# State-space kernel summed on TensorE, split gate product, and output products between gates, in the first stage of a decoder layer

## The chip, the cores and the metric

One core of a Trainium2 chip runs the whole program. The metric is the device time in microseconds of one execution; the median of three runs is given, and one further execution was profiled.

## What is computed

The program is one decoder layer on x of 8 batches x 512 steps x 256: a state-space (Mamba) block, a cross attention over 64 context rows, and a mixture of experts. The change lies in the first block. Its convolution branch is multiplied by zero, so that the input of the recurrence is 1 everywhere:

```python
xc = xc * 0 + 1
dBC = xc @ W_x.T
delta = jax.nn.softplus(dlt @ W_dt.T + b_dt)
A = -jnp.exp(A_log)
h = dA * h + dBx          # step, dA = exp(d_t * A)
y = ys.transpose(1, 0, 2) + D_skip * xc
out = y * jax.nn.silu(z) @ W_out.T
```

So y depends on the step t and on the inner channel alone (512 channels, 16 states each): with rate r = delta * A and coefficient c = B * C * delta of a channel's states, y(t) is D plus the running sum over t of the sum over 16 states of c * exp(r * t). z = x_norm @ W_in differs by batch.

## The kernel before, in words

All work is in 128-partition tiles. A batch is four tiles of 128 steps (TB = 4), the model width two blocks of 128 (KD = 2), the inner width four (KE = 4). The first stage (the functions under `nc.Block()`, lines 214 to 561) is written out by hand as one instruction order for each engine, with semaphores between them. For every batch b it does this.

- VectorE takes the statistics (`stats_part`, L111 and L115), GpSimd the inverse deviation (`norm_rstd`, L120 and L122), and each of them normalises two tiles (`norm_apply`, L127). The normalised tiles `hn`, the statistics and the deviation have one buffer each.
- TensorE transposes them (`transposes`, L274), ScalarE copies the result to SBUF (`evac`, L479), and `z_part` (L287) makes z with plain fp32 matmuls. z is copied out by ScalarE for three of four blocks (L484) and by VectorE for the fourth (L420), and kept for all eight batches in `sz`.
- Beside it the state-space kernel is summed: 64 times (4 channel blocks x 16 states) ScalarE makes 511 exponentials (`pw`, L500) and VectorE adds them into `kern` with their coefficient (L424). A scan over `kern` then gives `yD` (L429).
- When all of z is there, TensorE makes the keys' values (L314, and L315 with the bias as a product of one row), then the output products: `out_part(b)` waits for the low part of the gated z. VectorE multiplies z (after silu) with `yD` (`gate`, L440), ScalarE makes the high part `gh` (`high`, L512), VectorE the low part `gl` (`low`, L141), TensorE 48 products of 256 columns (`product`, L135 to L137), VectorE adds them to x (`residual`, L436). Output banks are two, so batch b waits for the residual of batch b - 1.
- GpSimd then lays the keys out in blocks (`kbd`, L555) for the next stage.

A split operand is a pair of fp32r tensors, high and low; `product` multiplies such pairs in three matmuls (high by high, high by low, low by high). An fp32 matmul shows as two records in the trace.

The last instruction of the stage on VectorE is the second residual of batch 7. All engines meet there, and the attention stage begins.

## Time and profile before

| | us |
|---|---|
| median of 3 runs | 992.65 (989.8 to 994.75) |
| the profiled execution, own time | 989.96 |
| its span | 988.3 |
| TensorE busy (matmul) in the span | 923.4 |
| VectorE busy | 625.2 |
| ScalarE busy | 556.4 |
| GpSimd busy | 347.0 |

Busy time of a matmul includes its pipelined end, so that neighbours overlap and the spacing of their starts is the pace. "Idle before" in a row is the time for which the engine had nothing to do, with what ended it. The first stage ends at about 166 us; the lines changed by the edit are all in it, save the preparation of inputs on the host.

### The profile page before, as it was taken

The numbers are of one execution on the slowest core, as the hardware profiler recorded it, in microseconds if no ns is written. First come the engines' busy times: TensorE is split into PE (matmuls) and PEld (weight loads), VectorE is DVE, ScalarE is ACT, GpSimd is POOL, SyncE is SP. The second block draws the span as 40 slices with busy tenths as digits, with TensorE's granted clock in tenths as the row PEclk, the third lists the DMA queues.
The fourth block names the chain that finished last, engine by engine and source line by source line (L and its number), as shares of the span: only waits on it lengthen the run. The fifth ranks groups of instructions, "written<-read, shape, count | busy, mean of one in ns | idle before, by whom it ended". The sixth has DMA issues, their size and how long they took to land.

```text
span 988.3 us, 20180 instructions
## 1 busy us (share of the span) xinstructions
PE 923.4 (93%) x6832; PEld 792.9 (80%) x6833; DVE 625.2 (63%) x1485; ACT 556.4 (56%) x1109; POOL 347.0 (35%) x323
## 2 busy tenths in 40 slices
PE   2998898799999889999999999999999999999996
PEld 2444697455666468888888889999999999999996
DVE  4898897566775666666665566546565646565453
ACT  3688842365545454444644467557565657565552
POOL 3652723222120235555555322424233332423222
PEclk9999999999999999999999999999999999999998
DMA  9200002000000201111112843534325252523222
GB/s 254 92 1 1 1 1 72 21 1 1 1 1 1 94 1 67 68 67 67 68 67 76 264 116 94 134 49 107 66 44 131 42 140 44 130 42 54 44 44 33
DMA packets 49312, 64.21 MB, mean 65 GB/s; under 512 B 10289, under 2 KB 42290, under 8 KB 49138
## 3 DMA queue, kind: packets, MB, share of 16 engines
q0 software_dynamic: 17504, 34.87, 15.2%
q1 hardware_dynamic: 31618, 27.68, 9.6%
q10 hardware_dynamic: 144, 1.05, 0.4%
q8 instruction: 28, 0.46, 0.2%
q14 instruction: 18, 0.15, 0.1%
HBM read 38.82 MB, written 24.77 MB: 64 GB/s over the span
## 4 chain that ended last, share of the span: by engine, by line
PE 71%; DVE 7%; ACT 3%; issue 1%; DMA 0%; POOL 0%; SPq 0%; DVEq 0%; POOLq 0%; ACTq 0%
PE PS L135 20%; PE PS L136 19%; PE PS L137 19%; PE PS L646 3%; DVE mxpad L897 2%; PE PS L1559 2%; PE PS L687 2%; PE PS L673 2%; PE PS L693 1%; ACT recs L802 1%; ACT prT L783 1%; PE PS L1109 1%; DVE mxT L908 1%; DMA xr<-routed_rows 0%; DVE hidl L141 0%
## 5 line engine op out<-in xcount | busy, mean ns | idle before, releaser
L1605 ACT ACTIVATE hideh<-PS,be 128x256 fp32r<-128x256 f32 x280 | 140.5, 502 | 152.4 <-PE PS L137 152.4
L1633 POOL DMA_INDIRECT out_rows<-y,toki x70 | 122.3, 1747 | 268.3 <-DVE y L1673 259.1
L141 DVE TENSOR_TENSOR hidel<-act32e,hideh 128x256 fp32r<-128x256 f32 x280 | 118.4, 425 | 107.9 <-ACT act32e L1607 107.6
L135 PE MATMUL PS<-xTeh,wfch 128*128 128x256 f32 x560 | 159.4, 285 | 2.2 <-issue 1.1
L136 PE MATMUL PS<-xTel,wfch 128*128 128x256 f32 x560 | 158.5, 283 | 0.0
L137 PE MATMUL PS<-xTeh,wfcl 128*128 128x256 f32 x560 | 158.4, 283 | 0.0
L135 PE MATMUL PS<-wprh,hideh 128*128 128x256 f32 x560 | 157.9, 282 | 0.0
L137 PE MATMUL PS<-wprh,hidel 128*128 128x256 f32 x560 | 154.8, 277 | 0.0
L136 PE MATMUL PS<-wprl,hideh 128*128 128x256 f32 x560 | 154.8, 277 | 0.0
L1607 ACT ACTIVATE act32e<-PS,be 128x256 f32<-128x256 f32 x280 | 140.9, 503 | 2.8 <-DVE hidel L141 2.8
L135 PEld LDWEIGHTS PS<-xTeh,wfch 128*128 128x128 f32 x560 | 107.3, 192 | 3.8 <-issue 2.3
L137 PEld LDWEIGHTS PS<-xTeh,wfcl 128*128 128x128 f32 x560 | 107.5, 192 | 0.0
L136 PEld LDWEIGHTS PS<-xTel,wfch 128*128 128x128 f32 x560 | 107.3, 192 | 0.0
L136 PEld LDWEIGHTS PS<-wprl,hideh 128*128 128x128 f32 x560 | 105.3, 188 | 0.0
L135 PEld LDWEIGHTS PS<-wprh,hideh 128*128 128x128 f32 x560 | 105.2, 188 | 0.0
L137 PEld LDWEIGHTS PS<-wprh,hidel 128*128 128x128 f32 x560 | 105.2, 188 | 0.0
L1218 ACT ACTIVATE hidh<-PS,bfs 128x512 fp32r<-128x512 f32 x64 | 44.2, 690 | 57.8 <-PE PS L137 54.2
L120 POOL TENSOR_TENSOR vare<-mv,small 128x4 f32<-128x4 f32 x24 | 9.0, 376 | 189.4 <-DVE mv L115 189.2
L1291 POOL DMA_INDIRECT routed_rows<-rows,slotc x64 | 65.5, 1024 | 24.9 <-issue 19.3
L135 PE MATMUL PS<-wpsh,hidh 128*128 128x256 f32 x256 | 73.5, 287 | 0.3 <-DVE hidl L141 0.3
L137 PE MATMUL PS<-wpsh,hidl 128*128 128x256 f32 x256 | 72.1, 282 | 0.0
L136 PE MATMUL PS<-wpsl,hidh 128*128 128x256 f32 x256 | 72.1, 282 | 0.0
(254 smaller groups left out, 2165.3 us busy)
## 6 DMA issues: line engine op xcount, KB each, us to landing
xr<-routed_rows SPq DMA_DIRECT2D x36, 272.0 KB, 2.8
fcraw<-in_Wfc POOLq DMA_DIRECT2D x8, 1024.0 KB, 6.0
prraw<-in_Wproj POOLq DMA_DIRECT2D x8, 1024.0 KB, 8.6
X<-in_x SPq DMA_DIRECT2D x8, 512.0 KB, 6.1
out_rows<-X SPq DMA_DIRECT2D x8, 512.0 KB, 3.0
routed_rows<-pads SPq DMA_DIRECT2D x8, 272.0 KB, 4.5
out_rows<-y,toki POOLq DMA_INDIRECT x70, 3.8
ctx<-in_ctxT SPq DMA_DIRECT2D x4, 256.0 KB
```

The costliest lines, as they stand in the source:

```text
L135: nc.tensor.matmul(out, wh, xh, start=first, stop=False)
L136: nc.tensor.matmul(out, wh, xl, start=False, stop=False)
L137: return nc.tensor.matmul(out, wl, xh, start=False, stop=last)
L141: return eng.tensor_tensor(out, whole, high.bitcast(F32), ALU.subtract)
L646: last = nc.tensor.matmul(at, qT[rows, b % 2, m, t * P:(t + 1) * P], kbd[rows, b, m, :].rearrange("p (i n) -> p i n", i=2), start=m == 0, ...
L673: nc.tensor.matmul(PS[:, j, :], kbd[rows, b, m, j % 2 * P:(j % 2 + 1) * P], qT[rows, b % 2, m, :], start=True, stop=False, skip_group_chec ...
L687: last = nc.tensor.matmul(PS[32 * j:32 * j + 32, 2, :], onesbd[:, m, :], prT[:, m, j, :], start=m == 0, stop=m == KD - 1, skip_group_check ...
L1218: nc.scalar.activation(hid[0][:, j, :], PS[:, j % 4, :], ACT.Gelu_apprx_tanh, bias=bfs[:, j:j + 1])
L1291: nc.gpsimd.indirect_dma_start(out=RG, out_offset=bass.IndirectOffsetOnAxis(ap=slotc[:, t, m:m + 1], axis=0), in_=rows[:, t, :], in_offset ...
L1605: nc.scalar.activation(hid[0][:, j, :], PS[:, j % 4, 0:BLK], ACT.Gelu_apprx_tanh, bias=bias)
L1607: nc.scalar.activation(act32[:, j % 2, :], PS[:, j % 4, 0:BLK], ACT.Gelu_apprx_tanh, bias=bias).then_inc(h_ready, 1)
L1633: nc.gpsimd.indirect_dma_start(out=out, out_offset=bass.IndirectOffsetOnAxis(ap=toki[:, h:h + 1], axis=0), in_=y[:, h, :], in_offset=None, ...
```

## The change

The state-space kernel is no longer made state by state. exp(r t) is factored as exp(r (t mod 64)) times exp(r 64 (t div 64)): `powers` holds 64 + 8 exponentials for each of 64 channel groups (8 channels x 16 states on the partitions), made from products with `steps` (`arguments` on VectorE, `powers_exp` on ScalarE, four chunks). `columns` puts the coefficient and a mask of the channel in. 64 matmuls (`kernel_sums`) contract over the 128 partitions, ScalarE copies the sums out (`kernel_rows`), and 32 transposes (`kernel_turn`) bring channels onto partitions; `response` scans from PSUM. The z product takes split operands (`winp`; `hTh` by ScalarE, `hTl` by VectorE in `x_low`). z of batches 4 to 7 is made after the output products of batches 0 to 3, in five buffers instead of eight; batches 3 to 7 take silu straight out of PSUM. VectorE's rounds begin with the residual. The value bias is folded into the bias `bo` by two matmuls at the end. x of batch 0 is loaded first. VectorE normalises three of four tiles of the first five batches. The key blocks lie between GpSimd's rounds.

```diff
-        SLOT = KE * NS // B
-        PWB = 4
+        NE = P // NS
+        G = EI // NE
+        GH = G // 2
+        NA = 8
+        NB = L // NA
+        SLOTS = 5
+        BY_DVE = [3] * 5 + [2] * (B - 5)
...
+            CHUNKS = [slice(16 * i, 16 * (i + 1)) for i in (0, 2, 1, 3)]
+            COPIED = 3
...
-                    for dst, src in ((wx[:], d["W_xT"].rearrange("(k p) r -> p k r", p=P)),
-                                     (wdt[:], d["W_dtT"]), (bdt[:], d["b_dt"]), (dsk[:], d["D_skip"]),
-                                     (alog[:], d["A_log"].rearrange("(k p) n -> p k n", p=P)),
-                                     (steps[:], d["steps"])):
-                        sp.dma_start(dst, src).then_inc(w_in, 16)
                     x_load(0)
                     for dst, src in ((ident[:], d["ident"]), (small[:], d["small"])):
                         sp.dma_start(dst, src).then_inc(consts_in, 16)
+                    for dst, src in ((wx[:], d["W_xT"].rearrange("(k p) r -> p k r", p=P)),
+                                     (wdt[:].rearrange("r e g -> r (e g)"), d["W_dtT"]), (bdt[:], d["b_dt"]),
+                                     (dsk[:], d["D_skip"]), (alog[:], d["A_log"]), (steps[:], d["steps"])):
+                        sp.dma_start(dst, src).then_inc(w_in, 16)
...
-                    def z_part(b):
-                        pe.wait_ge(hT_ready, KD * b + KD)
-                        for e in range(KE):
+                    def z_part(b, parts=range(KE)):
+                        pe.wait_ge(hT_low, KD * b + KD)
+                        for e in parts:
                             if b:
-                                if e < KE - 1:
-                                    pe.wait_ge(z_copied[0], (KE - 1) * (b - 1) + e + 1)
-                                else:
-                                    pe.wait_ge(z_copied[1], b)
+                                pe.wait_ge(z_copied, KE * (b - 1) + e + 1)
+                            if b == 3 and e < KD:
+                                pe.wait_ge(kT_ready, e + 1)
+                            if b == 3 and e >= KD:
+                                pe.wait_ge(yD_ready, 2)
+                            if b == 4:
+                                pe.wait_ge(v_ready, 4 * (e + 1))
                             for k in range(KD):
-                                last = nc.tensor.matmul(PS[:, e, :], win[:, k, e * P:(e + 1) * P],
-                                                        hT[:, b % 2, k, :], start=k == 0, stop=k == KD - 1)
+                                last = product(PS[:, e, :], [w[:, k, e * P:(e + 1) * P] for w in winp],
+                                               [x[:, b % 2, k, :] for x in (hTh, hTl)], k == 0, k == KD - 1)
                             last.then_inc(z_psum, 1)
 
-                    pe.wait_ge(consts_in, 32)
-                    transposes(0)
...
-                    for b in range(B):
-                        z_part(b)
-                        if b < B - 2:
-                            transposes(b + 2)
...
+                    def kernel_sums(half):
+                        pe.wait_ge(cU_ready, 2 * half + 2)
+                        if half:
+                            pe.wait_ge(ksb_ready, half)
+                        for q in range(GH // 2):
+                            for j in range(2):
+                                g = GH * j + GH // 2 * half + q
+                                last = nc.tensor.matmul(PS[NB * j:NB * (j + 1), 6 + q // 8, q % 8 * NB:(q % 8 + 1) * NB],
+                                                        powers[:, g, 0:NB], cU[:, g, :], start=True, stop=True,
+                                                        skip_group_check=True)
+                        last.then_inc(raw_psum, 1)
+
+                    def kernel_turn(half):
+                        pe.wait_ge(ksb_ready, half + 1)
+                        bank = (2, 6)[half]
...
+                        for a in range(NA):
+                            for j in range(2):
+                                rows = slice(NB * j, NB * (j + 1))
+                                last = nc.tensor.transpose(PS[:, bank + j, a * NB:(a + 1) * NB], ksb[rows, half, a, :],
+                                                           ident[rows, rows])
+                        last.then_inc(kern_psum, 1)
...
+                    transposes(0)
+                    pe.wait_ge(dlt_ready, 1)
+                    for e in range(NE):
+                        last = nc.tensor.matmul(PS[0:G, 6, 8 + e:9 + e], wdt[:, e, :], dlt[:], start=True, stop=True)
+                    last.then_inc(small_mm, 1)
+                    pe.wait_ge(win_split, 2)
+
+                    def z_and_transposes(b):
+                        z_part(b, range(KE - 1))
+                        transposes(b + 1)
+                        z_part(b, range(KE - 1, KE))
+
+                    z_and_transposes(0)
+                    pe.wait_ge(rates_ready, 1)
+                    for i, src in enumerate((rate, coef)):
+                        last = nc.tensor.transpose(PS[:, 7, P + G * i:P + G * (i + 1)], src[:], ident[0:G, 0:G])
+                    last.then_inc(small_mm, 1)
+                    z_and_transposes(1)
+                    kernel_sums(0)
+                    z_and_transposes(2)
+                    kernel_sums(1)
+                    keys()
+                    kernel_turn(0)
+                    kernel_turn(1)
+                    z_and_transposes(3)
+                    values()
                     for b in range(B):
                         out_part(b)
+                        if b + 5 < B:
+                            transposes(b + 5)
+                        if b + 4 < B:
+                            z_part(b + 4)
+                    pe.wait_ge(bv_ready, 1)
+                    for k in range(KD):
+                        last = nc.tensor.matmul(PS[:, 0, 0:D], bv[:, k, :], wo[:, k, :], start=k == 0, stop=k == KD - 1)
+                    last.then_inc(bo_psum, 1)
...
+                    def x_low(b):
+                        if b >= 2:
+                            dve.wait_ge(z_psum, KE * (b - 1))
+                        for k in range(KD):
+                            dve.wait_ge(hT_high, KD * b + k + 1)
+                            low(nc.vector, hTl[:, b % 2, k, :], PS[:, 4 + k, :], hTh[:, b % 2, k, :]).then_inc(hT_low, 1)
+
+                    def arguments(i):
+                        gs = CHUNKS[i]
+                        nc.vector.tensor_tensor(powers[:, gs, :],
+                                                rcT[:, 0, gs].unsqueeze(2).to_broadcast([P, 16, NB + NA]),
+                                                steps[:].unsqueeze(1).to_broadcast([P, 16, NB + NA]),
+                                                ALU.mult).then_inc(prod_ready, 1)
+
+                    def columns(i):
+                        gs = CHUNKS[i]
+                        dve.wait_ge(powers_ready, i + 1)
+                        nc.vector.tensor_tensor(cU[:, gs, :].rearrange("p g (a e) -> p g a e", e=NE),
+                                                cmask[:, gs, :].unsqueeze(2).to_broadcast([P, 16, NA, NE]),
+                                                powers[:, gs, NB:].unsqueeze(3).to_broadcast([P, 16, NA, NE]),
+                                                ALU.mult).then_inc(cU_ready, 1)
+
+                    def response(half):
+                        dve.wait_ge(kern_psum, half + 1)
+                        bank = (2, 6)[half]
+                        for j in range(2):
+                            k = 2 * j + half
+                            nc.vector.tensor_tensor_scan(yD[:, k * L:(k + 1) * L], onesrow[:], PS[:, bank + j, :],
+                                                         dsk[:, k:k + 1], ALU.mult, ALU.add).then_inc(yD_ready, 1)
 
...
+                    x_low(1)
+                    stats_part(2)
+                    dve.wait_ge(small_mm, 3)
+                    link(nc.vector.tensor_copy(rcT[:].rearrange("p i g -> p (i g)"), PS[:, 7, P:P + 2 * G]))
+                    arguments(0)
+                    apply_part(2)
+                    arguments(1)
+                    link(nc.vector.tensor_tensor(cmask[:], rcT[:, 1, :].unsqueeze(2).to_broadcast([P, G, NE]),
+                                                 emask.unsqueeze(1).to_broadcast([P, G, NE]), ALU.mult))
+                    stats_part(3)
+                    columns(0)
+                    columns(1)
+                    x_low(2)
+                    arguments(2)
+                    apply_part(3)
+                    arguments(3)
+                    stats_part(4)
+                    columns(2)
+                    columns(3)
+                    x_low(3)
+                    apply_part(4)
+                    response(0)
+                    response(1)
                     dve.wait_ge(yD_ready, KE)
+                    stats_part(5)
                     gate(0)
+                    dve.wait_ge(wout_split, 1)
+                    low(nc.vector, wouts[1][:], wout[:], wouts[0][:]).then_inc(wout_split, 1)
+                    gate(1)
+                    x_low(4)
+                    gate_low(0)
+                    gate(2)
                     for b in range(B):
-                        if b < B - 1:
-                            gate(b + 1)
-                        dve.wait_ge(g_high, b + 1)
-                        low(nc.vector, gl[:, b, :], sz[:, b, :], gh[b % 2][:]).then_inc(g_low, 1)
                         if b:
                             residual(b - 1)
+                        if b + 5 < B:
+                            apply_part(b + 5)
+                        if b + 3 < B:
+                            gate(b + 3)
+                        if b + 1 < B:
+                            gate_low(b + 1)
+                        if b + 6 < B:
+                            stats_part(b + 6)
+                        if b == 4:
+                            dve.wait_ge(late_in, LATE_IN)
+                            nc.vector.tensor_copy(causal16[:], causal[:])
+                            nc.vector.tensor_copy(ident16[:], ident[:])
+                            nc.vector.tensor_copy(bv[:], bvc[:].unsqueeze(2).to_broadcast([P, KD, P])).then_inc(bv_ready, 1)
                         if b == B - 2:
-                            dve.wait_ge(x1_ready, 2 + 2)
+                            for half in hn_ready:
+                                dve.wait_ge(half, B)
                             norm_stats(link, tiles(0)).then_inc(hn_var, 1)
-                        if b == B - 1:
-                            dve.wait_ge(hn_rstd, 2 * B + 2)
-                            norm_apply(0)
+                        if b + 5 < B:
+                            x_low(b + 5)
+                    dve.wait_ge(hT_psum, B)
+                    dve.wait_ge(hn_rstd, 2 * B + 2)
+                    norm_apply(0)
                     residual(B - 1)
-                    dve.wait_ge(x1_ready, 2 * B + 2)
+                    dve.wait_ge(bo_psum, 1)
+                    nc.vector.tensor_tensor(bo[:], bo[:], PS[:, 0, 0:D], ALU.add).then_inc(bo_ready, 1)
+                    dve.wait_ge(x1_ready, 2 * B)
```

TensorE's queue from its third group of products on, before. `PS` is PSUM, `hT` the transposed x, `win` the weights of z, `ctx` the context, `wk` the key weights.

```order
L263 MATMUL PS<-dlt,wdt 128x1 x4
L274 MATMUL PS<-ident,hn 128x128 x16
L287 MATMUL PS<-hT,win 128x512 x8
L274 MATMUL PS<-ident,hn 128x128 x8
L287 MATMUL PS<-hT,win 128x512 x8
L274 MATMUL PS<-ident,hn 128x128 x8
L304 MATMUL PS<-ctx_79,wk 128x512 x4
L287 MATMUL PS<-hT,win 128x512 x8
```

And now, TensorE around the second half of the sums (between z of batch 2 and z of batch 3):

```order
L137 MATMUL PS<-hTh,winl 128x512
L302 MATMUL PS<-cU,powers 64x64 x32
L326 MATMUL PS<-ctx_79,wk 128x512 x4
L317 MATMUL PS<-ident,ksb 128x64 x32
L135 MATMUL PS<-hTh,winh 128x512
```

Sixteen transposes stood together ahead of the first z; now eight do, and the sums, the keys and the turning transposes stand between z products (the first half of the sums, 32 more, stands between z of batches 1 and 2).

VectorE in the output rounds, before. `sz` is the gate product, `gl` the low part, `X` the residual.

```order
L440 TENSOR_TENSOR sz<-sz,yD 128x2048
L141 TENSOR_TENSOR gl<-sz,gh_101 128x2048
L436 TENSOR_TENSOR X<-X,PS 128x512 x2
L440 TENSOR_TENSOR sz<-sz,yD 128x2048
L141 TENSOR_TENSOR gl<-sz,gh_100 128x2048
L436 TENSOR_TENSOR X<-X,PS 128x512 x2
```

And now, one round of batches 1 to 2 and the beginning of the next:

```order
L459 TENSOR_TENSOR X<-X,PS 128x512 x2
L127 TENSOR_SCALAR hn<-X,mv,rstd 128x256 x2
L466 TENSOR_TENSOR sz<-sz,yD 128x2048
L141 TENSOR_TENSOR gl<-sz,gh_90 128x2048
L111 BN_STATS stats<-X 128x6 x4
L115 BN_AGGR mv<-stats 128x2 x4
L141 TENSOR_TENSOR hTl<-PS,hTh 128x512 x2
L459 TENSOR_TENSOR X<-X,PS 128x512 x2
```

The residual stands first, and normalising, statistics and the low part of a later batch's x lie in the round.

## Rows read from the trace of the kernel before

**Rows 1.** Stretches of z and output products: length, PE, PEld, DVE, ACT, POOL busy, PEclk.
```profile
28.20:97.60 69.40, 66.64 (x187) 32.25 (x186) 61.23 (x129) 56.82 (x99) 32.14 (x24) 0.98 0.05 16
...
112.40:164.90 52.50, 49.68 (x384) 48.92 (x384) 42.80 (x40) 26.03 (x20) 20.36 (x18) 0.94 0.00 1
```

**Rows 2.** Timeline to 30 us: start us, us, engine line op out<-in xcount [idle before].
```profile
0.89 0.46 SPq L225 DMA_DIRECT2D wx<-in_W_xT  x1
...
4.14 0.43 SPq L218 DMA_DIRECT2D X<-in_x  x1
...
6.54 1.01 PE L255 MATMUL PS<-ones,wx 128*64 128x1 f32 x8 [6.54 <-DMA steps<-in_steps]
...
7.48 1.91 PE L258 MATMUL PS<-wx,ones 128*128 128x32 f32 x8
...
12.29 1.40 DVE L111 BATCH_NORM_STATS2 stats<-X 128x6 f32<-128x256 f32 x4
...
19.76 1.94 PE L274 MATMUL PS<-ident,hn 128*128 128x128 f32 x8 [8.26 <-DVE hn L127]
...
21.74 1.08 ACT L479 ACTIVATE hT<-PS 128x512 f32<-128x512 f32 x2 [2.93 <-PE PS L274]
...
26.52 1.94 PE L274 MATMUL PS<-ident,hn 128*128 128x128 f32 x8 [4.81 <-POOL hn L127]
...
28.25 8.00 PE L287 MATMUL PS<-hT,win 128*128 128x512 f32 x16
```

**Rows 3.** DMA issues, weights of z: KB, us from issue to landing.
```profile
win<-in_W_inT SPq DMA_DIRECT2D x1, 512.0 KB, 5.1
```

**Rows 4.** Timeline of TensorE, 30 to 84 us.
```profile
36.96 7.03 PE L287 MATMUL PS<-hT,win 128*128 128x512 f32 x16
43.83 1.04 PE L274 MATMUL PS<-ident,hn 128*128 128x128 f32 x8
44.70 3.60 PE L304 MATMUL PS<-ctx,wk 128*128 128x512 f32 x8
...
81.26 1.83 PE L274 MATMUL PS<-ident,hn 128*128 128x128 f32 x8 [2.76 <-issue]
```

**Rows 5.** Timeline of TensorE, values and output products, 97 to 165 us.
```profile
99.16 1.13 PE L314 MATMUL PS<-wv,ctx 128*128 128x256 f32 x4
100.22 0.69 PE L315 MATMUL PS<-bv,ones 1*128 1x256 f32 x2
100.85 1.13 PE L314 MATMUL PS<-wv,ctx 128*128 128x256 f32 x4
...
112.49 0.55 PE L135 MATMUL PS<-wouth,gh 128*128 128x256 f32 x1 [1.46 <-DVE gl L141]
...
122.21 0.42 PE L135 MATMUL PS<-wouth,gh 128*128 128x256 f32 x1 [2.43 <-DVE X L436]
...
159.02 0.36 PE L135 MATMUL PS<-wouth,gh 128*128 128x256 f32 x1
...
164.69 0.28 PE L137 MATMUL PS<-wouth,gl 128*128 128x256 f32 x1
```

**Rows 6.** Timeline of TensorE, split products of 512 columns in the next stage.
```profile
188.70 0.39 PE L136 MATMUL PS<-hTbl,wqh 128*128 128x512 f32 x1
...
190.99 0.39 PE L137 MATMUL PS<-hTbh,wql 128*128 128x512 f32 x1
```

**Rows 7.** Groups and timeline of VectorE and GpSimd in the first stage.
```profile
L424 DVE SCALAR_TENSOR_TENSOR kern<-pw,coef,kern 128x511 f32<-128x511 f32 x64 | 45.2, 754 | 5.2 <-ACT pw L500 5.1
L436 DVE TENSOR_TENSOR X<-X,PS 128x512 f32<-128x512 f32 x16 | 10.9, 683 | 5.6 <-PE PS L137 5.5
...
118.77 2.70 DVE L141 TENSOR_TENSOR gl<-sz,gh 128x2048 fp32r<-128x2048 f32 x1
...
138.21 2.29 DVE L141 TENSOR_TENSOR gl<-sz,gh 128x2048 fp32r<-128x2048 f32 x1
...
104.22 25.24 POOL L555 TENSOR_TENSOR kbd<-kT,small 128x256 f32<-128x256 f32 x16 [23.06 <-DVE yD L429]
```

437 lines of the change are left out of this document (230 added, 207 removed).

## The prediction

> **What bounds the kernel now.** I first cut the first stage into stretches [rows 1]. TensorE is busy for 66.64 us of the 69.40 us in which z is made, and for 49.68 us of the 52.50 us in which the output products run. Its ends decide the stage; VectorE is second, with 42.80 us of the same 52.50. Later stages share no edited line, and they start when the block's last residual has landed, so what the first stage gains or loses should reach the end of the program whole.
>
> Then the timeline of the first 30 us [rows 2]: TensorE has its first two small groups behind it by 9.4 us, but the first z product starts only at 28.25. The tiles of x are asked for at 4.14, behind six weight loads of which the first goes out at 0.89; VectorE works on the step sizes first, takes the statistics of batch 0 at 12.29, transposes come at 19.76, the copy at 21.74, and z(0) still waits for the transposes of batch 1 at 26.52, though the weights of z, asked for three places behind x, took only 5.1 us to land [rows 3], so by about 10.7.
>
> Then TensorE in the z part [rows 4]. From z at 36.96 to the next transposes at 43.83 are 6.87 us for 16 records, two for one fp32 matmul of 512 columns: **0.859 us each**. Eight transposes take 43.83 to 44.70, 0.87 us or 0.109 each. The keys take 3.6. At 81.26 there is a wait of 2.76 us, and the transposes behind it take 1.83 instead of 1.04: half pace. So 8 x 6.87 + 6 x 0.87 + 3.4 = 63.6 us of dense work fill 69.3 (28.25 to 97.58), and 5.7 are lost.
>
> Then the values and output products [rows 5]: a batch of values is 1.06 us (99.16 to 100.22) and its bias product, one row deep, 0.63 more (to 100.85). The first output product waits 1.46 us for VectorE's low part, another 2.43 for a residual (122.21), where the residual stood behind a gate product and a low part in VectorE's queue. Output products without a wait run from 159.02 to 164.69, 47 spacings of **0.12 us**. So 384 of them are 46.1 us of dense work in 52.5: 6.4 lost to those waits and the half pace behind them.
>
> **The change part by part.** TensorE is all but continuously busy before and, by what follows, after; so I sum what TensorE does and what it waits for.
>
> *The start.* x of batch 0 is now first in SyncE's queue, 3.25 us (4.14 less 0.89) earlier; VectorE takes its statistics before anything else. The six weight loads behind it arrive later by about the same, and TensorE's small products with them; they no longer hold batch 0 up. Statistics at 5, 1.8 us; GpSimd's two small steps about 1.9; three tiles on VectorE 1.2: transposes at about 10.5, over at 12.4 (1.94 at this pace, [rows 2]). The weights of z land at 10.7, are copied by ScalarE (1.0) ahead of the copy of x (1.08), low parts on VectorE cost 1.2 and 1.3, the softplus chain 0.7 between them. z(0) starts at about 16 where it was 28.25: **-12.2 us**. Bounds 14.5 to 19.
>
> *z in three products.* A 512-column product of split operands recurs every 0.229 us (188.70 to 190.99, ten spacings, [rows 6]). 64 x (0.859 - 3 x 0.229) = **-11.0 us**. The split costs VectorE sixteen low parts, counted below.
>
> *The value bias* leaves TensorE: 8 x 0.63 = **-5.0**. In exchange two fp32 matmuls and an addition stand at the end: the products take about 1.06 (a batch of values) and the add 0.4, of which the last residual covers 0.7: **+0.8**.
>
> *The state-space kernel.* 64 updates on VectorE (45.2 us, [rows 7]) and as many exponentials on ScalarE go. In come 64 sums on TensorE, fp32, 64 stationary and 64 moving columns. The trace has none of that size. Low end: the 64-column group that starts at 6.54 spends 0.117 us a record at half pace, so 0.059 at full pace and 0.12 a sum, 7.5 us. High end: 128 columns with 32 moving, the group at 7.48, 0.239 a record, 30.6 us if even half pace stays. Transposes of 128 by 128 at full pace are 0.109 a record [rows 4]; these sums are half as wide and half as long, and two records are needed. I take 0.08 a record, 0.16 a sum: **+10.2**. The 32 turning transposes load 128 columns: 0.109 each, **+3.5** (1.7 to 7.8). Two transposes of rates +0.3. The Trainium skill, "TensorE: Matmul & The Clock Gate", section "LDWEIGHTS (loading the stationary operand)", makes a load last the column count over 1.2 GHz: 53 ns for 64 columns, an estimate of 6.8 us for the 128 records. By it the sum would be 3.4 us better (973 where I say 976). No row here shows such loads back to back at full pace.
>
> *Inside the stretch now:* transposes of batch 1, ahead of z before: +0.9. Work of TensorE between first z and last product: -11.0 - 5.0 + 10.2 + 3.5 + 0.3 + 0.9 = **-1.1**.
>
> *What is lost to waits.* Before: 5.7 + 1.5 (ahead of the first output product) + 6.4 = 13.6. After, (a) slow pace behind the start: 2. (b) Ahead of the first sums: from 16 VectorE has three rounds of statistics (1.8 each), two of normalising (1.2), one low part of x (1.3), the small chain (2.9), two arguments of 1152 elements (1.2 each, by the 2.29 us of 2048 elements, [rows 7]), the mask 0.7 and two columns products of 1.1, with two waits for GpSimd of 1: together 19 to 20; it is ready at 35 to 36, where TensorE's z(0), z(1), sixteen transposes and slow start end at 31.5 to 32: 3.5 to 4 in all, spread over three waits. (c) From the turned kernel to the first output product VectorE has four scans 4.8, statistics 1.8, two gates 4.5, weight low 1.2, x low 1.3, low part 2.2 = 15.8, TensorE z(3) 5.5, transposes 0.9 and values 8.5 = 14.9: 1, and 1.5 for pace. (d) In the rounds TensorE has 5.8 + 0.9 + 5.5 = 12.1 us while VectorE has residual 1.4, apply 0.8, gate 2.3, low 2.3, statistics 1.8 and x low 1.3 = 9.9 [rows 2, 7]: covered, and the residual no longer stands behind a gate. From round 4 on it is 5.8 against 5.9, with a lead from before: 0 to 2. Sum 10: **-3.6**.
>
> **Sum:** -12.2 - 1.1 + 0.8 - 3.6 = -16.1 us. The profiled execution took 989.96 us (span 988.3), near the lower of the runs shown; their median is 992.65. Own time less 16.1 is 973.9; from the median, 976.6. I say 976.
>
> Costed at nothing: GpSimd's key blocks (25.24 us, 104.22 on) now lie between its rounds, wanted by the next stage only; the three early silu passes of ScalarE are hidden while TensorE does z(3); five buffers instead of eight for z bind only if a copy waits for output product b-5, done long before. Moved loads (W_out ahead of x of batch 4) are needed 30 us after they land.
>
> **Rivals.**
>
> *VectorE paces.* Chance 0.17. If VectorE's steps last a tenth or more longer than I have them, the wait ahead of the sums passes 1.4 us in one piece and the sums run at half pace as products did after 1.46 and 2.43 [rows 5]. Price: 1 to 3 of wait, 5 of pace, and 2 to 4 at the first output product: 8 to 11. The time is 984 to 988. For it: with GpSimd busy on key blocks from 104.22 to 129.5, VectorE's low part takes 2.70 instead of 2.29 [rows 7], and GpSimd now works beside it for most of the stage. Against it: only a part of the steps have two inputs that meet GpSimd. The Trainium skill, "SBUF — State Buffer", section "Who interferes with whom", says that a VectorE operation with both inputs in SBUF and a GpSimd one that reads there block each other for whole instructions; by that rule arguments, columns, gates and low parts can each lose a GpSimd tile. The trace agrees in direction: 2.70 against 2.29.
>
> *Sums dear, at full pace.* Chance 0.1. At 0.24 to 0.3 us a sum they cost 5 to 9 more: 981 to 985.
>
> *Slower than before.* Chance 0.04. If sums and turns run like the group at 7.48 (0.239 a record throughout, at half pace), sums cost 30.6 instead of 10.2 and turns 7.8 instead of 3.5: +24.7, in all +8.6, 1001 us. It decides from 0.41 us a sum on (16.1 + 10.2 over 64). Against it: row 7.48 is from the first microseconds of the program, and here z products run right before.
>
> *Change hides elsewhere.* Chance 0.04: the next stage waits for loads issued at its own beginning and gives the gain back, 988 to 997. Its first rows wait for products and reductions, not for DMA, so I hold it low.
>
> *Better than forecast:* sums at their low end and no wait but the slow start: 967 to 971, inside my own case.
>
> **How the numbers follow.** The forecast has 0.65; within it 968 to 983. Range: low end by start at 14.5, sums at 7.5 and losses 6 (-24 from the median); high end takes in the VectorE rival for the most part: 967 to 986. About 0.5% (5 us) is what a measurement of this kernel can tell from no change; below 987.7 is faster: 0.92. Slower by that, above 997.6: 0.04. The rest 0.04.
>
> **What would show it.** In the profile after: first z product near 16 us; z products recurring every 0.23; a group of 64 x 2 sum records in which one is near 0.08; first output product at 73 to 78 and the stage's last residual at 147 to 152 instead of 165; no wait over 1 us between output products. Wrong if z starts after 19, if a wait over 1.4 stands before the sums with half pace behind it, or if output products wait for low parts.

## The result, and the profile after

The changed kernel takes 969.49 us, the median of four runs (968.24 to 970.98); the kernel before, run beside it, 993.62 (989.8 to 994.75). The ratio is **0.976** with a 95% interval of 0.973 to 0.980. The forecast was 976.0, with a range of 967 to 986: the time lies inside it, 6.5 us under the forecast. The profiled execution took 969.2 us (span 967.4) against 989.96 (988.3).

First, where in the program the time went. The next stage begins with VectorE's statistics at line 111, right behind the stage's last addition. In the trace of before they start at 166.41 us. The timeline of TensorE in the changed kernel there:

```profile
142.45 1.03 PE L398 MATMUL PS<-wo,bv 128*128 128x256 f32 x4
```

and of VectorE:

```profile
142.65 0.69 DVE L459 TENSOR_TENSOR X<-X,PS 128x512 f32<-128x512 f32 x1 [2.17 <-PE PS L137]
143.51 0.42 DVE L574 TENSOR_TENSOR bo<-bo,PS 128x256 f32<-128x256 f32 x1 [0.17 <-PE PS L398]
144.44 1.41 DVE L111 BATCH_NORM_STATS2 stats<-X 128x6 f32<-128x256 f32 x4 [0.51 <-PEq L231]
```

They start at 144.44, so **the first stage is 22.0 us shorter**, and what follows takes 823.0 us (967.4 less 144.44) where it took 821.9. Among the kernels below, all with the same later stages, that later part scatters from 819.9 to 826.5 us. So I read an experiment's effect on the first stage from the start of these statistics (the *stage end*), and use whole times for verdicts only. One trace stands for each kernel, so it matters how well traces of the same instructions agree. In seven kernels whose start is that of the change, the first z product comes at 15.89 to 16.39. In three whose program is the same up to the first output product, that product comes at 68.31, 69.38 and 69.55. In six that are the same from there on, the rest of the stage takes 74.87 to 74.91 us. The changed kernel's own trace is the late end of both scatters, so a stage end that differs from it by little more than 1 us says nothing. The whole times of the kernels that lie 2 to 5 us above 969.49 would not tell them from the changed kernel by themselves.

The stage in stretches (length, then busy us and count of PE, PEld, DVE, ACT and POOL, then PEclk, DMA share, GB/s), to be held against [rows 1]:

```profile
16.40:60.00 43.60, 38.44 (x296) 30.08 (x297) 33.71 (x80) 25.20 (x33) 15.67 (x12) 0.96 0.35 105
60.00:84.00 24.00, 22.43 (x136) 19.80 (x135) 23.21 (x30) 17.38 (x32) 21.96 (x13) 1.00 0.01 1
84.00:144.00 60.00, 57.45 (x411) 53.65 (x409) 39.94 (x54) 18.90 (x22) 18.90 (x18) 1.00 0.00 1
```

TensorE still decides. But from 60 to 84 us VectorE is busy for 23.21 of 24 us and GpSimd for 21.96: around the first output product the three are level. The groups of TensorE that the change added or moved, in order of time:

```profile
16.39 0.77 PE L135 MATMUL PS<-hTh,winh 128*128 128x512 f32 x1 [2.14 <-DVE hTl L141]
...
31.72 1.07 PE L275 MATMUL PS<-ident,hn 128*128 128x128 f32 x8 [1.75 <-DVE hn L127]
...
37.21 3.38 PE L302 MATMUL PS<-cU,powers 128*64 128x64 f32 x64 [3.04 <-DVE cU L442]
...
47.33 2.08 PE L302 MATMUL PS<-cU,powers 128*64 128x64 f32 x64
49.34 3.70 PE L326 MATMUL PS<-ctx,wk 128*128 128x512 f32 x8
52.98 1.21 PE L317 MATMUL PS<-ident,ksb 64*128 64x64 f32 x32
...
62.08 7.17 PE L335 MATMUL PS<-wv,ctx 128*128 128x256 f32 x32 [1.28 <-ACT sz L592]
69.55 0.36 PE L135 MATMUL PS<-wouth,gh 128*128 128x256 f32 x1 [0.29 <-DVE gl L141]
...
123.82 0.36 PE L135 MATMUL PS<-wouth,gh 128*128 128x256 f32 x1 [0.89 <-DVE X L459]
...
136.66 0.36 PE L135 MATMUL PS<-wouth,gh 128*128 128x256 f32 x1 [1.14 <-DVE X L459]
```

Read it against [rows 2, 4, 5]. The first z product comes at 16.39, where it was 28.25. A group of 64 records of sums takes 2.08 us at full clock (granted 1.00 from 47.3 to 49.4, the upper of the clock's two levels; 0.50 is the lower, and "half pace" means it); the first group took 3.38, with a granted clock of 0.50 from 38 to 41. The first output product comes at 69.55, where it was 112.49. There is no wait over 1.2 us between output products.

### The profile page after: what moved, and what is told of

Same layout as the page of the kernel before. It is cut to its first block, busy times and chain, and to the rows that moved or that the text cites. A ratio compares the mean times of both kernels' runs of the same rounds, so it can differ in the third digit from the quotient of the medians.

```text
span 967.4 us, 20474 instructions
## 1 busy us (share of the span) xinstructions
PE 911.7 (94%) x7054; PEld 805.9 (83%) x7055; DVE 596.1 (62%) x1437; ACT 522.2 (54%) x1057; POOL 339.8 (35%) x318
## 3 DMA queue, kind: packets, MB, share of 16 engines
q0 software_dynamic: 17504, 34.87, 15.6%
## 4 chain that ended last, share of the span: by engine, by line
PE 73%; DVE 7%; ACT 3%; issue 1%; DMA 0%; POOL 0%; SPq 0%; DVEq 0%; POOLq 0%; ACTq 0%
PE PS L135 21%; PE PS L136 20%; PE PS L137 20%; PE PS L797 3%; DVE mxpad L1048 2%; PE PS L1710 2%; PE PS L838 2%; PE PS L824 2%; PE PS L844 1%; ACT recs L953 1%; ACT prT L934 1%; PE PS L1260 1%; DVE mxT L1059 1%; DVE hidl L141 0%; PE PS L805 0%
```

## The experiments

The stage end of the changed kernel, 144.44, is what the figures are held against. Beside these kernels, in the same three sets of runs, the kernel before took 992.7, 991.0 and 992.3 us.

### What a sum costs

**Sums twice.** Every sum is issued a second time, with the same result.

```
-                        for q in range(GH // 2):
+                        for q in [q for _ in range(2) for q in range(GH // 2)]:
```

> The changed kernel with each of the 64 sums issued twice (same operands, same place; the output stays the same). Theory A (TensorE's own work sets the stage, every record of the sums lies on its path): 128 more records, at the 0.032 us a record of the second group and up to 0.052 of the first, so 4.1 to 5.5 us longer than the changed kernel: about 974 to 975. Rival B (VectorE's steps pace the first half of the stage, the sums are hidden beside them): less than 1.5 us longer. The price I had forecast (0.08 a record) would make it 10 longer.

Measured: 973.46 us, ratio 0.981 (0.978 to 0.985); stage end 147.80, 3.4 later, though its first z product was 0.4 sooner. The two groups:

```profile
36.78 5.50 PE L302 MATMUL PS<-cU,powers 128*64 128x64 f32 x128 [3.05 <-DVE cU L442]
...
48.80 3.95 PE L302 MATMUL PS<-cU,powers 128*64 128x64 f32 x128
```

Each has 64 records more than in the changed kernel and takes 2.12 and 1.87 us more (5.50 less 3.38, 3.95 less 2.08): 4.0 us together, and 3.4 to 3.8 of them reach the end of the stage, a little under the 4.1 to 5.5 expected. The sums lie on the path, and are cheap: **0.03 us a record**, where I had taken 0.08.

**One half, then the other.** The sums with j = 0 write partitions 0 to 63 of PSUM, those with j = 1 partitions 64 to 127. Each uses 64 of the array's 128 columns; I call the two the column halves. The change alternates them; this kernel does one half first.

```
-                        for q in range(GH // 2):
-                            for j in range(2):
+                        for j in range(2):
+                            for q in range(GH // 2):
```

> The changed kernel with the two loops inside kernel_sums exchanged, so that 16 sums into the lower 64 output partitions come first and 16 into the upper 64 behind them, where they alternated. Theory A (a sum is cheap because two neighbours that use different halves of the array's columns run side by side): the spacing of records goes from 0.032 to about 0.06 and each group of 64 records from 2.0 to about 3.8 us: 3.5 to 5 us longer. Rival B (a product of 64 by 64 simply takes 0.032 a record whatever stands beside it): no difference, both groups as before.

Measured: 972.31 us, ratio 0.981 (0.976 to 0.986); stage end 148.03, 3.6 later.

```profile
37.47 5.29 PE L302 MATMUL PS<-cU,powers 128*64 128x64 f32 x64 [3.05 <-DVE cU L442]
...
49.26 3.77 PE L302 MATMUL PS<-cU,powers 128*64 128x64 f32 x64
```

The same 64 records take 3.77 us instead of 2.08 (0.059 a record against 0.032), and 5.29 instead of 3.38 in the group behind the wait (mean granted clock 0.68 and 0.56 there, so this pair is the less clean one). So neighbours on different halves run side by side, and that is why the sum was mis-sized: my low end, 0.059 a record, was the price of one half at a time. The Trainium skill, "TensorE: Matmul & The Clock Gate", section "LDWEIGHTS (loading the stationary operand)", gives 53 ns for 64 columns. The group with one half at a time agrees (59 ns), the alternating one does not (32 ns). The same page's section "The mechanism" has weight loads overlap matmuls only where the row groups differ. Here the rows are the same and the columns differ, and the records overlap all the same. "TensorEngine Tiling (Array Packing)", section "Key Properties", says that different tiles load and multiply in parallel and that each is tied to its own PSUM partitions, and with the first the trace agrees.

### The start and the first half

**x behind the weights.** The load of x of batch 0 goes back behind the six small weight loads, the old order.

```
-                    x_load(0)
...
                         sp.dma_start(dst, src).then_inc(w_in, 16)
+                    x_load(0)
```

> The changed kernel with the six weight loads ahead of x of batch 0 in SyncE's queue, as before. Theory A (the first tiles of x start the chain to the first z product): x lands some 3 us later, about 1.5 to 3 us of it reach the first z product (16.4 to 18 or 19) and the end. Rival B (the weights of z and the small products are as late, so the order of the loads does nothing): less than 1 us, first z product at 16.4.

Measured: 971.77 us, ratio 0.979 (0.976 to 0.982); first z product 19.43 (3.04 later), stage end 147.77 (3.3 later). Of the 11.9 us of the start, 3 come from the place of x in SyncE's queue, and they reach the end whole. The next experiment is on the other 9.

**Transposes of batch 1 first**, the old order of TensorE, the rest as changed.

```
-                    z_and_transposes(0)
+                    transposes(1)
+                    z_part(0)
```

> The changed kernel with the transposes of batch 1 ahead of z of batch 0, as before, instead of ahead of its last block. Theory A (z of batch 0 need not wait for batch 1, and that is most of the 9 us of earlier start that the order of the loads does not explain): first z product at 23 to 24 instead of 16.4; some of it comes back, since TensorE then waits less ahead of z of batch 1 and of the sums: 3 to 6 us longer. Rival B (VectorE paces up to the sums, whose columns products are ready at 37 whatever TensorE does before): less than 1.5 us longer.

Measured: 974.71 us, ratio 0.982 (0.979 to 0.985); stage end 149.87, 5.4 later.

```profile
21.43 1.94 PE L275 MATMUL PS<-ident,hn 128*128 128x128 f32 x8 [7.57 <-POOL hn L127]
23.02 0.78 PE L135 MATMUL PS<-hTh,winh 128*128 128x512 f32 x1
```

TensorE stands idle for 7.57 us for a tile of batch 1; for the last 5.6 of them everything for z(0) is there, since its last low part ends at 15.9. z starts 6.6 later, and 1.2 of that comes back. So the interleave of transposes into z is worth 5.4 us, the largest part of the start.

**z in fp32**, as before the change: one product of two records instead of three split ones. The low parts of x and of W_in go too.

```
-                                last = product(PS[:, e, :], [w[:, k, e * P:(e + 1) * P] for w in winp],
-                                               [x[:, b % 2, k, :] for x in (hTh, hTl)], k == 0, k == KD - 1)
+                                last = nc.tensor.matmul(PS[:, e, :], win[:, k, e * P:(e + 1) * P],
+                                                        hTh[:, b % 2, k, :], start=k == 0, stop=k == KD - 1)
```

> The changed kernel with z made by plain fp32 matmuls as in the kernel before; neither the weights nor the transposed x are split, so VectorE loses sixteen low parts of x and one of the weights (11.4 us) and ScalarE one copy. Theory A (TensorE's work sets the stage): 11.0 us more of dense work, less the 2.5 us in which z waited for low parts and some of the 3.0 us ahead of the sums: 6 to 9 us longer, 976 to 979. Rival B (VectorE paces the first half, so what it is spared comes back): between 2 shorter and 2 longer.

Measured: 972.85 us, ratio 0.980 (0.976 to 0.983); stage end 147.74, **3.3 later where the products are 11.0 us longer**. Between both theories. The waits of TensorE that are left in this kernel's stage (us in total, times, longest), and its sums:

```profile
PE PS L135 <- DVE X L459: 2.4, 2, 1.6
PE PS L302 <- DVE cU L442: 2.1, 1, 2.1
```
```profile
33.82 3.22 PE L302 MATMUL PS<-cU,powers 128*64 128x64 f32 x64 [2.06 <-DVE cU L442]
```

Without low parts z(0) starts at 13.81 instead of 16.39 (2.6), the sums wait 1.0 less, and the waits for hn (1.8), for ScalarE ahead of the values (1.3) and for the second low part (0.4) are gone. That is 7.1 of the 7.7 us that came back. Where they came back tells more: the first output product stands at 66.89, which is 2.7 *sooner* than in the changed kernel, and from there to the stage end it is 80.85 us instead of 74.89, 6.0 longer. So the split costs 2.7 us up to the first output product, where its low parts hold back z(0) and the sums, and all of its gain lies in the rounds behind, where four batches of z are 5.5 us shorter. Together that is the 3.3. A kernel that splits only the z of batches 4 to 7 was not tried.

**Two tiles each.** VectorE normalises two of four tiles of every batch instead of three, GpSimd two.

```
-        BY_DVE = [3] * 5 + [2] * (B - 5)
+        BY_DVE = [2] * B
```

> The changed kernel with VectorE and GpSimd normalising two tiles each in all batches (the change gives VectorE three of four in batches 0 to 4). Theory A (GpSimd's tile, 1.2 us alone and up to 2.6 beside VectorE, is the longer branch ahead of the transposes): transposes of batches 1 to 3 wait 1 to 2.5 us longer each, 3 to 6 us longer in all, with hn by GpSimd as the releaser. Rival B (VectorE is the bound there, and each tile it is spared saves 0.4 us): 0 to 2 shorter.

Measured: 972.47 us, ratio 0.979 (0.976 to 0.982); stage end 146.18, 1.7 later.

```profile
34.97 1.17 PE L275 MATMUL PS<-ident,hn 128*128 128x128 f32 x8 [3.88 <-issue]
39.23 2.08 PE L302 MATMUL PS<-cU,powers 128*64 128x64 f32 x64 [0.53 <-DVE cU L442]
...
49.09 2.09 PE L302 MATMUL PS<-cU,powers 128*64 128x64 f32 x64 [1.19 <-DVE cU L442]
```

The wait ahead of the sums falls from 3.04 to 0.53, and the transposes ahead of them wait 3.88 instead of 1.75. The row names no releaser, but GpSimd's two tiles for them end at 34.87, just before. The first z product is 0.7 later too (17.05), since GpSimd's second tile of batch 0 ends at 11.03. VectorE's wait became GpSimd's, with a small loss. The direction is the one expected, the size is under it, and it is not far above what two traces of the same program differ by.

### Where the residual stands in VectorE's queue

**Residual after the gate.** Only the residual moves, from the head of each round behind the other steps.

```
                     for b in range(B):
-                        if b:
-                            residual(b - 1)
                         if b + 5 < B:
...
                             gate_low(b + 1)
+                        if b:
+                            residual(b - 1)
```

> The changed kernel with the residual behind apply, gate and low part in each of VectorE's rounds, as in the kernel before. Theory A (with z of a later batch between output products TensorE does not ask for the residual in the first four rounds; only rounds 5 to 7 do): 1 to 4 us longer, all of it between output products after 117 us. Rival B (the place of the residual is what took the lost 6.4 us of the output stretch away): 6 or more longer, with waits in the early rounds too. Rival C: no difference, since VectorE has time in every round.

Measured: **1013.47 us, ratio 1.021 (1.018 to 1.024)**; stage end 191.40, 47 later. One line's place turns a gain of 2.4% into a loss of 2.1%, and of my numbers only Rival B's open "6 or more" holds; none was near. The waits of TensorE, and from the timeline the first output product of one round:

```profile
PE PS L135 <- DVE X L459: 35.2, 6, 6.7
```
```profile
109.09 0.55 PE L135 MATMUL PS<-wouth,gh 128*128 128x256 f32 x1 [6.70 <-DVE X L459]
```

VectorE in that round:

```profile
90.13 0.38 DVE L115 BATCH_NORM_AGGREGATE mv<-stats 128x2 f32<-128x6 f32 x4
97.64 1.29 DVE L141 TENSOR_TENSOR hTl<-PS,hTh 128x512 fp32r<-128x512 f32 x2 [7.13 <-ACT hTh L584]
98.84 0.85 DVE L127 TENSOR_SCALAR hn<-X,mv,rstd 128x256 f32<-128x256 f32 x2
103.06 2.67 DVE L466 TENSOR_TENSOR sz<-sz,yD 128x2048 f32<-128x2048 f32 x1 [3.37 <-ACT sz L592]
105.65 2.70 DVE L141 TENSOR_TENSOR gl<-sz,gh 128x2048 fp32r<-128x2048 f32 x1
108.27 1.27 DVE L459 TENSOR_TENSOR X<-X,PS 128x512 f32<-128x512 f32 x2
```

The residual's operands have long been there. It stands behind a gate that waits for ScalarE's copy of a z product, which TensorE has only just made. TensorE's next step, the output product, needs the residual; so it waits for ScalarE's last copy (about 0.7), gate 2.67, low part 2.70 and half a residual (0.7), together the 6.7 us of the row, with VectorE itself idle for 7.13 and 3.37 us in the same round. Nothing is short of capacity: **from 60 to 191 us VectorE is busy for 63.61 of 131 us**. The engines take turns instead of overlapping. The matmul behind the wait takes 0.55 instead of 0.36: half pace adds to each wait. From the first output product to the last, TensorE is busy for 84.85 us instead of 70.87, at a mean granted clock of 0.83 instead of 1.00. So of the 47 us some 33 are waits (35.2 against 2.0) and 14 are slow pace behind them. In the changed kernel, VectorE in the same place:

```profile
90.48 1.27 DVE L459 TENSOR_TENSOR X<-X,PS 128x512 f32<-128x512 f32 x2
91.67 0.73 DVE L127 TENSOR_SCALAR hn<-X,mv,rstd 128x256 f32<-128x256 f32 x2
94.62 2.54 DVE L466 TENSOR_TENSOR sz<-sz,yD 128x2048 f32<-128x2048 f32 x1 [2.22 <-ACT sz L592]
97.09 2.70 DVE L141 TENSOR_TENSOR gl<-sz,gh 128x2048 fp32r<-128x2048 f32 x1
```

The same gate waits 2.22 us for the same copy, but the residual is out before it.

**Residual between low part and gate.** Having seen this, I formed the theory of a ring (residual, output product, z, copy, gate or high part, residual) and tried the place that is behind the low part only.

```
+                        if b + 1 < B:
+                            gate_low(b + 1)
+                        if b:
+                            residual(b - 1)
                         if b + 3 < B:
                             gate(b + 3)
```

> The changed kernel with VectorE's round in the order apply, low part, residual, gate. Theory A (what ruined the order with the residual last is any wait ahead of it that ends only with this round's z: ScalarE makes the high part for this low part behind the copies of z of batch b+3, so the low part carries the same tie as the gate): a wait of 4 to 6 us for the residual ahead of each output product and 30 to 42 us longer than the changed kernel. Rival B (only the gate of batch b+3 carries it, the low part is ready early): within 3 us of the changed kernel.

Measured: 1012.03 us, ratio 1.021 (1.018 to 1.024); stage end 186.44, 42 later, as expected. The low part is no better a neighbour than the gate: it waits for ScalarE's high part, which stands behind the same copies.

```profile
86.57 0.55 PE L135 MATMUL PS<-wouth,gh 128*128 128x256 f32 x1 [5.96 <-DVE X L459]
```
```profile
103.10 2.29 DVE L141 TENSOR_TENSOR gl<-sz,gh 128x2048 fp32r<-128x2048 f32 x1 [5.20 <-ACT gh L608]
```

**Residual sooner in the kernel before**: low part, residual, gate instead of gate, low part, residual.

```
                     for b in range(B):
-                        if b < B - 1:
-                            gate(b + 1)
...
                             residual(b - 1)
+                        if b < B - 1:
+                            gate(b + 1)
```

> The kernel BEFORE with the residual moved ahead of the next gate product in VectorE's rounds (low part, residual, gate). Theory A (a residual first is only safe when the gates run several rounds ahead, as they do in the changed kernel): here the next gate would stand behind the residual, which waits for output product b-1, and gate 2.2, high part 1.9 and low part 2.2 with the residual's 1.3 are 7.6 us in a row where an output product takes 5.8: 8 to 14 us longer than before, with a wait for the low part ahead of each output product. Rival B (the place of the residual by itself took the 2.4 us wait): 2 to 4 us shorter.

Measured: 1000.56 us, ratio 1.010 (1.008 to 1.012); stage end 175.82, 9.4 later than the kernel before, as expected. VectorE:

```profile
134.65 2.29 DVE L141 TENSOR_TENSOR gl<-sz,gh 128x2048 fp32r<-128x2048 f32 x1 [1.98 <-ACT gh L512]
136.86 1.33 DVE L436 TENSOR_TENSOR X<-X,PS 128x512 f32<-128x512 f32 x2
138.11 2.28 DVE L440 TENSOR_TENSOR sz<-sz,yD 128x2048 f32<-128x2048 f32 x1
142.37 2.29 DVE L141 TENSOR_TENSOR gl<-sz,gh 128x2048 fp32r<-128x2048 f32 x1 [1.98 <-ACT gh L512]
```

There the gates are one batch ahead. Behind the residual, each makes gate, ScalarE's high part and low part one chain of 7.7 us (134.65 to 142.37), longer than TensorE's 5.8 a batch. So an earlier residual is no gain by itself. That it pays in the changed kernel because the gates run three batches ahead there fits both results, but is not shown: the changed kernel with fewer gates ahead was not tried.

### The split products alone

The kernel before, with z in three products, the low parts on VectorE, and all else as it was.

```
+    def x_low(b):
...
+            low(nc.vector, hTl[:, b % 2, k, :], PS[:, 4 + k, :], hT[:, b % 2, k, :]).then_inc(hT_low, 1)
...
-                                last = nc.tensor.matmul(PS[:, e, :], win[:, k, e * P:(e + 1) * P],
-                                                        hT[:, b % 2, k, :], start=k == 0, stop=k == KD - 1)
+                                last = product(PS[:, e, :], [w[:, k, e * P:(e + 1) * P] for w in winp],
+                                               [x[:, b % 2, k, :] for x in (hT, hTl)], k == 0, k == KD - 1)
```

> The kernel BEFORE with only the z product split in three (weights and transposed x split; sixteen low parts of x and one of the weights more on VectorE, one copy more on ScalarE). Theory A (the split pays only because the 64 kernel updates left VectorE): VectorE had 61.2 us of work in the 69.4 us of the z stretch and gets 10.5 us more, so it becomes the bound there, and the 11.0 us that TensorE is spared are given back: between 3 shorter and 4 longer than before. Rival B (TensorE's dense work sets the stage whatever VectorE has): 8 to 11 us shorter.

Measured: 995.59 us, ratio 1.005 (1.003 to 1.007); stage end 171.67, 5.3 later than the kernel before. That is no gain but a small loss, a little beyond the 4 us that Theory A allowed. The stretch of z, against the first of [rows 1], and three of TensorE's waits in the stage (us in total, times, longest):

```profile
28.20:97.60 69.40, 58.33 (x242) 45.25 (x241) 62.90 (x135) 51.30 (x88) 30.47 (x24) 0.93 0.06 18
```
```profile
PE PS L277 <- POOL hn L127: 11.4, 3, 5.8
PE PS L135 <- DVE gl L141: 4.8, 1, 4.8
PE PS L277 <- DVE hTl L141: 3.7, 1, 3.7
```

TensorE is busy 8.3 us less in it and spends them waiting: 5.6 us in two waits for GpSimd's tiles (the third, of 5.8, is the old one ahead of the first z product, 4.8 before), 3.7 for a low part and 1.8 for VectorE's other steps. The values start 3.0 later than before (100.57), and the wait of 4.8 stands ahead of the first output product, where it was 1.5. VectorE is busy for 62.90 of the 69.40 us: it has its 45.2 us of kernel updates [rows 7] and the low parts on top. I read from this that the 11.0 us of my second term exist only because the change first takes those updates off VectorE; only one placement of the low parts among the updates was tried.

### Two attempts at a better kernel

**Waits out.** Half of z(2) ahead of the first sums, the low part of batch 2 ahead of the columns, silu(2) later, and VectorE's steps for the tail in other rounds. The core of it:

```
+                    z_part(2, range(KE - 2))
                     kernel_sums(0)
-                    z_and_transposes(2)
+                    z_part(2, range(KE - 2, KE - 1))
+                    transposes(3)
+                    z_part(2, range(KE - 1, KE))
                     kernel_sums(1)
```

> The changed kernel with four changes of order and no other work: x low part of batch 2 ahead of the statistics and columns products on VectorE and the first 32 sums between z blocks of batch 2 on TensorE; the third silu pass behind the copies of z of batch 3 on ScalarE; the casts one round earlier; the early statistics of batch 0 for the next stage one round later. Theory A (TensorE's waits are path): the 3.0 us wait ahead of the sums and the half pace behind it (1.3), the 1.3 ahead of the values and the two of 0.9 and 1.1 ahead of output products go: 4 to 7 us shorter than the changed kernel, 963 to 966. Rival B (the waits only move to the next product, since VectorE is as busy as before): within 1.5 us of 969.5.

Measured: 968.53 us (964.29 to 968.74), ratio 0.976 (0.974 to 0.979), not to be told from the changed kernel's 969.49, where 963 to 966 was expected. Stage end 143.65, 0.8 sooner, which is inside the scatter of the traces.

```profile
36.69 0.50 PE L135 MATMUL PS<-hTh,winh 128*128 128x512 f32 x1 [1.83 <-DVE hTl L141]
40.77 2.08 PE L302 MATMUL PS<-cU,powers 128*64 128x64 f32 x64 [1.06 <-DVE cU L445]
...
48.44 2.09 PE L302 MATMUL PS<-cU,powers 128*64 128x64 f32 x64 [1.77 <-DVE cU L445]
```

One wait of 3.04 became three of 1.83, 1.06 and 1.77; both groups of sums now run at full pace, and still the first output product comes 1.1 later (70.66), behind a wait of 1.87 for its low part where the values had waited 1.28. The gain is the tail's: the two late waits for residuals, 2.0 us, are 0.2.

**Order after 60 us.** The low part of batch 0 ahead of gate 1, silu(2) behind the first high part, and the same two moves for the tail.

```
-                    gate(1)
                     x_low(4)
                     gate_low(0)
+                    gate(1)
                     gate(2)
```

> The changed kernel with four changes of order that lie behind 60 us only: the third silu pass behind the copies of z of batch 3 and the high part; the gate of batch 1 behind the low part of batch 0; the casts one round earlier; the early statistics of batch 0 one round later. The first half, where the earlier reordering only moved its waits, is left. Theory A (VectorE and ScalarE pace the first output product by their queues, which had a gate and a silu in them that nobody waited for; the late waits for residuals stand behind casts and statistics): first output product 1.3 to 2 us earlier than 69.55, no wait over 0.3 for residuals, 3 to 4 us shorter than the changed kernel. Rival B (waits move again): within 1.5 us.

Measured: 970.20 us, ratio 0.979 (0.976 to 0.981), also not to be told from it; stage end 147.13, 2.7 later. The values start at 60.54 without a wait and the first output product comes at 67.25, 2.3 sooner (1.1 sooner than the earliest of the three traces named above), and of the waits for residuals 0.2 us are left. Then TensorE:

```profile
77.75 1.94 PE L275 MATMUL PS<-ident,hn 128*128 128x128 f32 x8 [4.45 <-issue]
```

The row names no releaser, but GpSimd's tiles for these transposes end at 77.65. They run beside VectorE's gates, now back to back:

```profile
64.90 12.75 POOL L127 TENSOR_SCALAR hn<-X,mv,rstd 128x256 f32<-128x256 f32 x2 [0.31 <-POOL rstd L122]
```

No version clearly beats the changed kernel.

## Why the prediction held, and where it did not

| Step, from the prediction | Forecast, us | Measured, us |
|---|---|---|
| Start: first z product | -12.2 (at 16) | -11.9 (16.39) |
| z in three products | -11.0 | -11.0 (0.229 each, as taken) |
| Value bias off TensorE | -5.0 | -5.0 |
| 64 sums | +10.2 | +4.1 at full pace |
| 32 turns | +3.5 | +1.1 |
| Values at before's pace | 0 (8.5 us) | -1.3 (62.08 to 69.26: 7.2) |
| Transposes of batch 1, rates | +1.2 | +1.1 |
| Tail | +0.8 | +0.5 |
| Lost to waits and pace, 13.6 before | 10, so -3.6 | 13.4, so -0.2 |
| Sum | -16.1 | -22.6 |

The last row of losses is what is left of 16.39 to 142.45 us once each record is counted at its full-pace spacing. The sum is 0.6 from the 22.0 measured, which is as well as such rows can be read. Work came out 9.8 us shorter than forecast (sums 6.1, turns 2.4, values 1.3), and the losses 3.4 longer: **two errors of opposite sign, a third of the one hidden by the other**.

- **The start: right**, for the reason given. The experiments split it: 3.0 from the place of x, 6.6 from the interleave (5.4 at the stage end); the other 2.3 were not tried apart. Nor was the value bias (-5.0) tried by itself; that figure is the length of its rows in the kernel before.
- **z: right as a term, not as a cause of its own.** Alone on the old kernel it costs 5.3 us at the stage end; in the changed kernel it costs 2.7 in the first half and gives 6.0 in the second. The table's terms are therefore not separable, and the prediction treated them as if they were.
- **Sums and turns: the term was mis-sized by 8.5 us.** The step that failed is "these sums are half as wide and half as long, and two records are needed. I take 0.08 a record". It looked at the shape of one record, not at where its neighbour sits in the array. The low bound (7.5 us) was too high as well. The turns, too, alternate between two row halves, and 0.036 a record came where I took 0.109; that it is for the same reason was not tried apart. The rivals "sums dear" and "slower", with an outcome over 980, fall with this.
- **Losses: (a) right** (1.9 us of half pace behind the start; the pace is read from nine products that recur at 0.43 us, since the profile's granted clock says 1.00 in the first 20 us of both kernels). **(b) under-sized**: 5.2 us in three waits (3.04, 1.75, 0.36), where I had 3.5 to 4, and one of them long enough that the sums ran at half pace behind it (3.38 against 2.08), 1.6 us more. Of the rival "VectorE paces" that much came true; its 8 to 11 us did not, since the sums were so short. **(c)** 1.6 of wait and hardly any slow pace, against 1 and 1.5. **(d)** 2.0, the upper end. The last 1.1 are small gaps around the waits, for which I had nothing. The prediction also let half pace follow from a wait over 1.4 us. Behind the wait of 1.75 the transposes take 1.07, which is full pace, while in the kernel before half pace stands behind 1.46: the length of the wait alone does not tell.
- **The signs: four of six failed.** z at 16.39 and its products at 0.23 came as named. The record near 0.08 (0.032), the first output product at 73 to 78 (69.55), the last residual at 147 to 152 (142.65) and no wait over 1 us between output products (1.14) did not. And one of the signs of being wrong came true: a wait over 1.4, of 3.04 us, stands before the sums with half pace behind it. The time lies where "better than forecast" had it (967 to 971), but not for that reason: it asked for sums at their low end and no waits, and the sums were below that end and the waits were there. That the two errors offset each other was luck: with the losses as forecast the same work would have ended near 966 (969.5 less 3.4, an estimate), just under the range.
- **The residual: the number held and the reasoning did not.** The prediction calls the rounds "covered, and the residual no longer stands behind a gate", and rests that on 9.9 us of VectorE's work against 12.1 of TensorE's. The experiments with the residual elsewhere have the same work on both and lose 42 to 47 us. Amount of work says nothing there; the order does. No rival named this, and the profile of before had a hint of it: 2.43 us behind a gate and a low part [rows 5]. A second of the same kind, behind a step that waits for TensorE itself, would have been the mechanism of a slower rival with a real price.
- **Rival "change hides elsewhere": fell.** The later part took 823.0 against 821.9 us.

What stays open: how much of the first half's loss is VectorE against GpSimd. Each reordering moved the wait to another place and none removed it. A kernel in which GpSimd has no tiles at all beside VectorE's long steps was not tried, nor one with z split only where it pays, in batches 4 to 7.

## What to carry to other kernels

In a queue that is worked in order, ask of each step what it waits for and who waits behind it, before adding up its work. A step whose operands are old must not stand behind one that waits for the engine that needs it. That line's place was worth twice the whole change.

Making one engine's work shorter pays only as far as the next engine lets it. Here the same split of 11 us lost 5.3 on the old kernel and was worth 3.3 on the new one, all of it in the second half. Empty the second engine first.

Price a small matmul from a row whose neighbours use the same parts of the array; alternating halves nearly halves the price.

## What the runs showed of the hardware

- fp32 products with 64 stationary and 64 moving columns: 0.059 us a record on one column half, 0.032 when neighbours alternate between the halves. Which part overlaps, load or product, the records do not tell apart.
- GpSimd beside VectorE's long two-input steps is slowed by far more than VectorE. In the changed kernel two tiles of line 127 take 7.58 us beside gates, 2.58 later (the second row below is the second of those two tiles by itself):

```profile
65.00 7.58 POOL L127 TENSOR_SCALAR hn<-X,mv,rstd 128x256 f32<-128x256 f32 x2 [0.31 <-POOL rstd L122]
67.08 5.49 POOL L127 TENSOR_SCALAR hn<-X,mv,rstd 128x256 f32<-128x256 f32 x1
...
80.89 2.58 POOL L127 TENSOR_SCALAR hn<-X,mv,rstd 128x256 f32<-128x256 f32 x2 [0.31 <-POOL rstd L122]
```

With gates back to back the same two tiles took 12.75, five times as long. VectorE's gates in that stretch took 2.28, the price without a neighbour; only beside GpSimd's two-input products over key blocks did its low part take 2.70. By the Trainium skill, "SBUF — State Buffer", section "Who interferes with whom", each blocks the other for whole instructions. The trace agrees for GpSimd: each of these four tiles is over 1.0 to 1.1 us after VectorE's last gate or low part in a row, whatever comes next on VectorE, a normalising step, one that reads PSUM or nothing (changed kernel: 67.11 behind 66.00 and 72.57 behind 71.60; gates back to back: 72.48 behind 71.50 and 77.65 behind 76.64). One tile gets through in each such gap, so an order with fewer gaps costs GpSimd more. For VectorE it agrees much less.
